# Edge arrays padded and laid out by the host, destinations loaded first, four tiles counted in one matmul

## The reference

```
h   = relu(layernorm(x))                                # no learned scale
W_r = sum_b w_comp[r, b] * weight[b]                    # 32 x 8, 8 x 128 x 128
agg[n] = sum over edges e with dst[e] == n of  norm[e] * h[src[e]] @ W_type[e]
out = x + relu(agg + bias + h @ loop_weight)
```

## Time and profile before

| | us |
|---|---|
| runs before | 1162.27, 1157.90, 1160.69; median 1160.69 |
| the profiled execution | 1159.61 |
| its span in the profile | 1157.8 |
| PE / VectorE / ScalarE / GpSimd busy | 1084.4 / 1036.0 / 942.8 / 810.1 |

### The profile page before, as it was taken

How to read it: one execution, slowest core, us unless ns; L and a number is a source line. 1 busy time by engine, 2 the same in 40 slices (tenths; PEclk the granted TensorE clock), 3 DMA queues, 4 the chain that set the end, 5 groups by cost and what they waited for, 6 DMA issues and landing times. The chain is left out here.

```text
span 1157.8 us, 24700 instructions
## 1 busy us (share of the span) xinstructions
PE 1084.4 (94%) x5388; PEld 699.0 (60%) x5388; DVE 1036.0 (89%) x4391; ACT 942.8 (81%) x3334; POOL 810.1 (70%) x1387
## 2 busy tenths in 40 slices
PE   0399999999999999999999999999689999999997
PEld 0374444444444444444444444444289999999997
DVE  1429999999999999999999999999689999999995
ACT  0139999999999999999999999998468888888885
POOL 4018888888888888888888888886245555555553
PEclk9999999999999999999999999999889999999999
DMA  1102222222222222222222222221399999999993
GB/s 45 34 7 71 73 63 72 74 72 72 67 68 74 72 72 71 64 73 72 72 73 63 71 73 73 72 65 60 91 271 298 296 297 299 293 303 296 298 298 117
DMA packets 88393, 144.57 MB, mean 125 GB/s; under 512 B 17683, under 2 KB 56916, under 8 KB 88244
## 3 DMA queue, kind: packets, MB, share of 16 engines
q0 software_dynamic: 28224, 76.93, 22.8%
q1 hardware_dynamic: 60020, 66.07, 19.1%
HBM read 91.44 MB, written 51.49 MB: 123 GB/s over the span
## 5 line engine op out<-in xcount | busy, mean ns | idle before, releaser
L607 PE MATMUL y_ps<-w_all,hT 128*128 128x512 f32 x1568 | 704.6, 596 | 1.0 <-ACT hT L547 0.7
L607 PEld LDWEIGHTS y_ps<-w_all,hT 128*128 128x128 f32 x1568 | 284.1, 191 | 313.5 <-issue 287.7
L405 POOL DMA_INDIRECT xg<-x,idx x392 | 395.5, 1009 | 77.2 <-issue 50.0
L494 ACT ACTIVATE z<-y_ps,mix 128x128 f32<-128x128 f32 x784 | 245.3, 364 | 59.0 <-PE y_ps L607 52.1
L726 DVE SCALAR_TENSOR_TENSOR sum_b<-y_ps,mix,sum_b 128x128 f32<-128x128 f32 x784 | 266.5, 340 | 0.0
L381 POOL TENSOR_TENSOR u<-z 128x128 f32<-128x128 f32 x392 | 181.8, 464 | 76.2 <-ACT z L494 73.0
L443 POOL DMA_DIRECT2D out<-res x98 | 75.6, 771 | 131.7 <-DVE res L959 131.7
L726 DVE SCALAR_TENSOR_TENSOR sum_b<-y_ps,mix,z 128x128 f32<-128x128 f32 x392 | 137.1, 350 | 31.6 <-ACT z L490 9.7
L574 ACT ACTIVATE hw<-xw,shift,nrstd 128x128 f32<-128x128 f32 x392 | 161.5, 482 | 2.1 <-DVE shift L950 0.4
L661 PE MATMUL y_ps<-w_loop,hwT 128*128 128x128 f32 x782 | 152.4, 276 | 0.0
L662 PE MATMUL y_ps<-seg,pick 96*128 96x128 f32 x782 | 152.3, 276 | 0.0
(11 more groups left out here) (97 smaller groups left out, 1313.2 us busy)
## 6 DMA issues: line engine op xcount, KB each, us to landing
seg<-msgs SPq DMA_DIRECT2D x391, 96.8 KB, 4.0
msgs<-msg SPq DMA_DIRECT2D x98, 258.0 KB
xw<-x POOLq DMA_DIRECT2D x97, 256.0 KB, 5.9
out<-res POOLq DMA_DIRECT2D x97, 256.0 KB, 4.9
xg<-x,idx POOLq DMA_INDIRECT x392, 2.6
w_all<-L_gnn_weight SPq DMA_DIRECT2D x1, 512.0 KB, 5.3
src_all<-src SPq DMA_DIRECT2D x1, 194.5 KB
dst_i<-dst SPq DMA_DIRECT2D x1, 194.5 KB
```

Of the source, the lines that this page charges most:

```text
L405: nc.gpsimd.indirect_dma_start(xg[:, q, j, :], None, x, bass.IndirectOffsetOnAxis(ap=idx[:, q, j:j + 1], axis=0)).then_inc(s_gather[q * G ...
L494: ins = nc.scalar.activation(z[:, r, b, :], y_ps[r][:, b, :], ACT.Copy, scale=mix[:, q, j, b:b + 1])
L607: nc.tensor.matmul(y_ps[r][:, b0:b0 + B // 2, :], hT[:, q, j, :], w_all[:, b0:b0 + B // 2, :], start=True, stop=True).then_inc(done, 1)
```

## The change

1. The host pads src, dst, edge type and norm and lays them out as 128 x 392, builds dst_next (128 x 1) and the block matrix mix_weight (128 x 32). Each is loaded by one transfer of 128 rows. GpSimd's six fills go, and the waits for them.
2. SyncE issues src, type and norm, each on its own semaphore. ScalarE's queue issues dst, dst_next, w_all, w_loop, w_mix and bias. VectorE waits for dst and dst_next alone before the planes; the type cast comes later, just ahead of the first one-hot; GpSimd waits for norm before the first gain.
3. The ones of pick are written by ScalarE, from ones, after its DMA issues and before group 0's means; ScalarE no longer waits for dst_f. TensorE waits for them (s_ones) ahead of the node stage.
4. The counts take 98 matmuls. Each has 52 stationary columns (13 high values x 4 tiles) and 128 moving columns (32 low values x 4 tiles), the four tiles being 98 apart, into y_ps[2]. Its 52 x 128 sum holds the wanted products of equal tiles beside those of unequal ones; VectorE masks with same_tile and adds the four low columns, and one fp32 matmul with same_bin adds the four rows. VectorE does the mask between group 0's means and step 0 of the loop, and so waits for the counts there; the matmul follows TensorE's step 0; the sum is copied to hist after VectorE's step 0, and the product that overwrites y_ps[2] waits for that copy.

```diff
@@ sync
-            sp.wait_ge(s_padded, 1)
-            load_edges(sp, src_all, src, s_src)
-            sp.wait_ge(s_padded, 6)
-            load_edges(sp, dst_i, dst, s_edges)
...
+            sp.dma_start(src_all[:, :], src).then_inc(s_src, 16)
+            sp.dma_start(type_i[:, :], etype).then_inc(s_type, 16)
+            sp.dma_start(norm_all[:, :], norm).then_inc(s_norm, 16)
@@ gpsimd
-            nc.gpsimd.memset(src_all[:, :], 0).then_inc(s_padded, 1)
...
-            pool.wait_ge(s_src, 32)
+            pool.wait_ge(s_src, 16)
...
             def gains(g, q):
+                if is_before(g, 1):
+                    pool.wait_ge(s_norm, 16)
@@ scalar
-            act.wait_ge(s_floats, 1)
+            act.dma_start(dst_i[:, :], dst).then_inc(s_dst, 16)
+            act.dma_start(next_i[:, :], dst_next).then_inc(s_dst, 16)
+            act.dma_start(w_all[:, :, :], weight.rearrange("b d f -> d b f")).then_inc(s_weights, 16)
+            act.dma_start(w_loop[:, :], loop_weight).then_inc(s_weights, 16)
+            act.dma_start(w_mix[:, :], mix_weight).then_inc(s_weights, 16)
...
+            act.wait_ge(s_consts, 1)
+            nc.scalar.activation(pick[SEG_P:P, :, :, :, :].rearrange("p r j c n -> p (r j c) n"),
+                                 ones[SEG_P:P, :].unsqueeze(1).to_broadcast([P - SEG_P, NRING * G * CHUNKS, P]),
+                                 ACT.Copy).then_inc(s_ones, 1)
@@ tensor
-            for t in range(NT):
-                mm = count(t, t == 0, t == NT - 1)
+            for g in range(NG):
+                mm = nc.tensor.matmul(y_ps[RING - 1][0:HI * G, 0, :],
+                                      hi_hot[:, :, :].rearrange("p v (j g) -> p (v j) g", j=G)[:, :, g],
+                                      lo_hot[:, :, :].rearrange("p u (j g) -> p (u j) g", j=G)[:, :, g],
+                                      start=g == 0, stop=g == NG - 1)
             mm.then_inc(s_hist, 1)
...
+                elif j == RING - 1:
+                    pe.wait_ge(s_step, 10)
...
-            sweep(pe, NG - 1, step)
+            step(0, 0, 0)
+            pe.wait_ge(s_step, 9)
+            nc.tensor.matmul(y_ps[RING - 1][0:HI, G, 0:LO], same_bin[0:HI * G, :], hist4_sum[:, :],
+                             start=True, stop=True).then_inc(s_hist, 1)
+            sweep(pe, NG - 1, step, first=1)
@@ vector
-            nc.vector.memset(pick[SEG_P:P, :, :, :, :], 1.0)
...
-            dve.wait_ge(s_edges, 16 * 8)
-            nc.vector.tensor_copy(type_f[:, :], type_i[:, :])
...
+            def window_counts():
+                dve.wait_ge(s_dst, 32)
...
+            window_counts()
             for j in range(DV):
...
+            dve.wait_ge(s_type, 16)
+            nc.vector.tensor_copy(type_f[:, :], type_i[:, :]).then_inc(s_step, 1)
+            dve.wait_ge(s_step, 7)
             one_hot(0, 0)
             means(0, 0)
             dve.wait_ge(s_hist, 1)
+            nc.vector.tensor_tensor(hist4[:, :], y_ps[RING - 1][0:HI * G, 0, :], same_tile[0:HI * G, :],
+                                    ALU.mult).then_inc(s_step, 1)
+            dve.wait_ge(s_step, 8)
+            nc.vector.tensor_reduce(hist4_sum[:, :], hist4[:, :].rearrange("p (u j) -> p u j", j=G), AX_X,
+                                    ALU.add).then_inc(s_step, 1)
+            step(0, 0, 0)
+            dve.wait_ge(s_hist, 2)
+            nc.vector.tensor_copy(hist[:, :], y_ps[RING - 1][0:HI, G, 0:LO]).then_inc(s_step, 1)
+            sweep(dve, NG - 1, step, first=1)
```

More of the change, by code:

```diff
@@ L66, in is_before, with tiles_of, pad_node, build_layer @@
     return isinstance(g, int) and g < n
-def build_layer(nc, x, src, dst, etype, norm, weight, w_comp, loop_weight, bias, out):
-    N, D = x.shape
[L71 to L75, removed]
+def tiles_of(edges):
+    return -(-edges // (P * G)) * G
+def pad_node(nodes):
+    return -(-(-(-nodes // P) + 1) // LO) * LO * P - 1
+def build_layer(nc, x, src, dst, dst_next, etype, norm, weight, mix_weight, loop_weight, bias, out):
+    N, D = x.shape
+    NT = src.shape[1]
     NG = NT // G
     EP = NT * P
-    FULL_P, REST = E // NT, E % NT
+    B = weight.shape[0]
+    R = mix_weight.shape[0] // G
+    F = loop_weight.shape[1]
     NW = -(-N // P)
@@ L141, in build_layer @@
         bad = sb("bad", [P, 4])
+        hist4 = sb("hist4", [HI * G, LO * G])
+        hist4_sum = sb("hist4_sum", [HI * G, LO])
+        tile_n = sb("tile_n", [P, P], I32)
+        tile_p = sb("tile_p", [P, 1], I32)
+        tile_nf = sb("tile_nf", [P, P])
+        tile_pf = sb("tile_pf", [P, 1])
+        bin_p = sb("bin_p", [P, 1], I32)
+        bin_pf = sb("bin_pf", [P, 1])
+        same_tile = sb("same_tile", [P, P])
+        same_bin = sb("same_bin", [P, HI])
         hist = sb("hist", [HI, LO])
@@ L591, in _ @@
             pe.wait_ge(s_meta, 1)
-            def count(t, first, last):
-                return nc.tensor.matmul(mix_ps[0:HI, 256:256 + LO], hi_hot[:, :, t], lo_hot[:, :, t],
-                                        start=first, stop=last)
-            for t in range(NT):
-                mm = count(t, t == 0, t == NT - 1)
+            for g in range(NG):
[3 more added lines that the diff above has]
+                                      start=g == 0, stop=g == NG - 1)
             mm.then_inc(s_hist, 1)
-            pe.wait_ge(s_weights, 16 * (3 + G))
+            pe.wait_ge(s_weights, 16 * 4)
             def products(g, q, j):
@@ L713, in _ @@
[L713 to L721, removed]
@@ L722, in _ @@
-            nc.vector.tensor_reduce(bad[:, 0:1], falls[:, :], AX_X, ALU.max).then_inc(s_step, 1)
+            nc.vector.tensor_copy(tile_nf[:, :], tile_n[:, :])
+            nc.vector.tensor_copy(tile_pf[:, :], tile_p[:, :])
+            nc.vector.tensor_copy(bin_pf[:, :], bin_p[:, :]).then_inc(s_step, 1)
+            dve.wait_ge(s_step, 2)
+            nc.vector.tensor_scalar(same_tile[:, :], tile_nf[:, :], tile_pf[:, 0:1], None, ALU.is_equal)
+            nc.vector.tensor_scalar(same_bin[:, :], iota_n[:, 0:HI], bin_pf[:, 0:1], None, ALU.is_equal)
@@ L1004, with give, edge_rows @@
     arrays, args = {}, []
-    for name in _INS:
-        a = np.ascontiguousarray(inputs[name])
-        arrays[name] = a
-        args.append(nc.dram_tensor(name, a.shape, mybir.dt.from_np(a.dtype), kind="ExternalInput").ap())
+    def give(name, a):
+        arrays[name] = np.ascontiguousarray(a)
+        args.append(nc.dram_tensor(name, arrays[name].shape, mybir.dt.from_np(arrays[name].dtype),
+                                   kind="ExternalInput").ap())
+    N = inputs["x"].shape[0]
+    tiles = tiles_of(inputs["src"].shape[0])
+    def edge_rows(name, pad):
+        a = inputs[name].reshape(-1)
+        rows = np.full((P * tiles,), pad, a.dtype)
+        rows[0:a.shape[0]] = a
+        return rows.reshape(P, tiles)
+    dst = edge_rows("dst", pad_node(N))
+    dst_next = np.full((P, 1), pad_node(N), dst.dtype)
+    dst_next[0:P - 1, 0] = dst[1:P, 0]
+    w_comp = inputs["L0_gnn_w_comp"]
+    R, B = w_comp.shape
+    mix_weight = np.zeros((G * R, G * B), w_comp.dtype)
+    for j in range(G):
+        mix_weight[j * R:j * R + R, j * B:j * B + B] = w_comp
+    give("x", inputs["x"])
+    give("src", edge_rows("src", 0))
+    give("dst", dst)
+    give("dst_next", dst_next)
+    give("etype", edge_rows("edge_type_32", 0))
+    give("norm", edge_rows("edge_weight1", 0))
+    give("weight", inputs["L0_gnn_weight"])
+    give("mix_weight", mix_weight)
+    give("loop_weight", inputs["L0_gnn_loop_weight"])
+    give("bias", inputs["L0_gnn_h_bias"])
     args.append(nc.dram_tensor("out", inputs["x"].shape, F32, kind="ExternalOutput").ap())
```

87 lines of the change are left out of this document (46 added, 41 removed).

## The result

The changed kernel takes 1125.17 us (median of 4 runs, 1125.06 to 1125.72) against 1161.48 for the kernel before on the same chips: ratio 0.9698, 95% interval 0.968 to 0.9715. A second set of runs gave 0.9693 (0.9676 to 0.9711). That is 36.3 us less where 48.8 were forecast. The time lies 13.3 us above the forecast (1111.9) and outside the 1105 to 1118 that belonged to it; it is inside the wider range up to 1127, which was there for the rivals, and 1.2 us from rival 1 (1126.4).

What follows compares the result with a forecast made beforehand. TensorE bounds the message loop, transfers the node stage, a chain of waits the start. First product 47.5 us earlier plus 1.3 of clock, 48.8 off 1159.61, gives 1110.8, median 1111.9 us; forecast 1105 to 1118, wider range 1104 to 1127.

Steps and rivals of the forecast that it cites:

- rival 1: Count matmuls cost by column: counts 23.7 us, 13.2 later, clock gain lost, total 1126.4; chance 0.17 with its intermediate prices.
- Loads: Edge loads at the start: 128 rows in one transfer land 4.0 us after issue (3.2 to 5.3), dst at 4.9.
- Start of the counts: TensorE's first count, 9.5 us after dst lands at 4.9: at 14.4 instead of 48.79 us.
- rival 2: Gathers stop VectorE's one-hots at the start: eight of 0.94 us, counts 7.6 us later, total 1119.5; chance 0.07.
- Counts: TensorE's 98 count matmuls at 107 ns each: 10.5 us, ending at 24.9; bounds 5.9 and 23.7 us.
- From the counts to the first product: Transposes, w_mix matmul and evictions before the loop's first product: 3.07 us unchanged, first product at 28.0, 47.5 us earlier.
- The clock: First two tiles' products lose 2.7 us at 1.2 GHz; 0 to 2.7 us saved, 1.3 taken.
- rival 4: Message loop settles into a slower cadence than 7.59 us a group; at 0.6 us per group 1170; chance 0.02.
- rival 3: Host layout doesn't spread the loads: src and dst share 25 GB/s, dst 13.6 us later, total 1125.5; chance 0.04.
- Sum: Whole kernel: 47.5 us from the earlier first product plus 1.3 of clock, 48.8 us; median 1111.9 us.

Runs made afterwards that it cites:

- Experiment 6: Also rows127: changed kernel with each edge array loaded as 127 rows and 1 row, new order and queues kept; 1138.04 us, ratio 0.9816.
- experiment 8: Kernel counting four adjacent tiles per matmul, with GpSimd's gathers beyond group 0 held until VectorE's planes are done; 1106.76 us, ratio 0.9545.
- oldqueue: Changed kernel with all loads on SyncE's queue in the old order, VectorE also waiting for type and norm; 1126.03 us, ratio 0.9712.
- oldcount: Changed kernel with the 392 single-tile 13 x 32 count matmuls of the kernel before; 1126.40 us, ratio 0.9714.

## Why the prediction was right in direction and 13 us off

- **Loads: the mechanism right, the time partly by luck.** The wait ended at 4.83 us, forecast 4.9. But dst landed 3.1 us after issue, below my 4.0 and even my lower bound of 3.2, and what ended the wait was dst_next, issued 0.44 us later and landing after 3.6, a transfer that the sum left out. In the other executions with this order it ended at 4.70 to 5.72. Experiment 6 shows that the 128th row makes the loads short. The rule of the Trainium skill (DMA: Bandwidth & Descriptors, Why a DMA increments its semaphore by 16 and not by 1), 127 rows on one engine, agrees with the 25 GB/s at a DMA share of 0.07 and the 14.3 us in rows127.
- **Start of the counts: nearly.** 15.13 for 14.4. The planes took 8.46 us (6.67 to 15.13) instead of 7.83, and the integer steps ahead of them 0.2 more, while gathers were issued. This is rival 2 at a twelfth of its price (0.6 of 7.6 us): a gather beside the planes costs VectorE about 0.2 us (experiment 8), not its whole 0.94. What the rival said of the other side, gathers held up, happened to one gather that nobody waited for.
- **Counts: this step failed.** "I take 107 ns, 10.5 us" was 232 ns, 22.7 us: 12.2 of the 12.9 us by which the first product came later than forecast (40.89 for 28.0). The bound was right (by column, 23.7), and so was rival 1, whose 1126.4 is the measured time within 1.2. The counts took 22.7 us for its 23.7, and they began 0.7 us later than it had them, with 1.2 us of the clock gained that it wrote off. I chose by the nearest row in size, an fp32 row of contiguous columns, although the operand differed in the one thing that sets the price. The rows could have told more: 60.3 ns is 1.88 ns for each of 32 far columns, the contiguous row 0.83 for fp32. And the clock should have warned: the first 6 us of products raised it, 23.6 us of counts had not, so a count was not like the contiguous row that I priced it by. The rule in the Trainium skill that spoke against my choice (SBUF — State Buffer, Door 1: a penalty for each access that crosses to a new 16-byte line) holds here and has a size, 1.8 ns a line. What it says next, that 8 bf16 can be stepped over for free, doesn't hold for these moving operands: step 2 is free (57 ns), step 3 takes 88 and step 4 115.
- **From the counts to the first product: right,** 3.06 for 3.07; mix began 1.96 us after the counts' end and took 0.19; its first reader came at 43.07. VectorE's new wait cost nothing.
- **The clock: right by luck.** I took the middle of two bounds. The first two tiles' products take 4.97 us for 6.15 in the profiled execution, 1.2 gained, but 6.35 in a second execution of the same kernel. The other kernels with far counts of 52 and 128 columns have 5.07 (oldqueue) and 5.13 (rows127), oldcount 6.27; whether the wider counts bring the clock up sooner these few don't settle. With near columns the full 2.6 us are there, 3.54 us in both executions.
- **The loop (rival 4) and the loads' layout (rival 3):** neither happened; 7.59 us a group, 128 rows spread.
- **Sum.** Forecast 48.8. Less 12.2 (counts), 0.7 (start), 0.1 (clock) is 35.8, the shift of the second group in the profiled execution (34.1 in the second one); the runs have 36.3.

## What to carry to other kernels

Fewer matmuls over the same far-stepped columns cost nearly the same here: count the 16-byte lines that the moving operand touches before counting instructions, and choose which tiles share a matmul (adjacent ones, here) so that columns lie side by side. Look at the number of rows of a transfer before its bytes: 127 for 128 turned a 3 us load into one of 8, four times in a row. When two hypotheses fit one row equally (per instruction, per column), give them equal weight, and don't break the tie by a row that differs in the point at issue.

## What the runs showed of the hardware that I had not expected

- The price of far columns is the same at both clock levels (230 ns in a block that ran at a granted 0.87 over its first 5 us, and in one at 0.50), and the clock fell under a stream of them: it was 1.00 when block L606 began and 0.50 from 40 us on, but stayed at 1.00 through the block of step 4 (115 ns each).
- A stationary operand with far columns costs too, 92 ns for 52 of them, and hides beside the moving one when that is dearer (231 ns with both far, 230 with the moving one alone).
- VectorE's bf16 compares keep their speed with outputs in runs of 4 elements (2.30 us for 13 planes, 2.31 before; 32 in 6.20 for 6.18).
- A gather issued beside such compares either passes (0.94 to 1.18 us) and costs VectorE about 0.2 us, or is stuck until 0.12 to 0.13 us behind the last of them (3.75 to 6.99 us on GpSimd instead of 0.95).
